# Gated delta-rule attention and mixture of experts: two chains in flight over 16 states, newly ordered engine programs, projection weights split earlier with three buffers

## What is computed

```python
q = short_conv(x @ Wq, conv_q)      # 4 taps, then silu; likewise k and v, three of each per token and head
beta = 2.0 * sigmoid(x @ Wb); g = -exp(A_log) * softplus(x @ Wa + dt_bias)
q = l2norm(q) * d ** (-0.5); k = l2norm(k)
def step(S, (qt, kt, vt, bt, gt)):  # one token; S is 128 x 128 for each sequence and head
    S = S * exp(gt)
    for i in range(3):
        kS = kt[i] @ S
        S = S + bt[i] * outer(kt[i], vt[i] - kS)
    return S, qt @ S
o = o * rsqrt(mean(o * o) + 1e-05) * rms_weight * silu(x @ Wg)
x = layernorm(x + o @ Wo);  x = layernorm(x + experts(x))
```

## Time and profile before

| | us |
|---|---|
| median of 3 runs (lowest, highest) | 5084.51 (5080.6, 5097.39) |
| the profiled execution, its own time | 5080.19 |
| its span | 5078.4 |
| of it setup, up to the barrier | 132.1 |
| of it middle loop, up to the experts' first transfer | 3959.6 |
| experts | 986.7 |
| busy: PE, PEld, DVE, ACT, POOL | 4474.4, 3959.6, 3659.4, 3570.6, 1354.3 |

### The profile page before, as it was taken

One profiled execution on the slowest core, in us unless ns is written; L12 is line 12 of the kernel. 1 busy time (PEld: TensorE's weight loads), 2 busy tenths in 40 slices (PEclk: granted clock), 3 DMA queues, 4 the chain that ended last, 5 costly groups with the idle time before them and its releaser, 6 DMA issues. The chain is left out here.

```text
span 5078.4 us, 150544 instructions
## 1 busy us (share of the span) xinstructions
PE 4474.4 (88%) x50436; PEld 3959.6 (78%) x50436; DVE 3659.4 (72%) x9814; ACT 3570.6 (70%) x8898; POOL 1354.3 (27%) x1231
## 2 busy tenths in 40 slices
PE   1799999999999999999999999999999966599991
PEld 0688888888888888888888888888888845488881
DVE  3788888878888878888888888788888722344445
ACT  2688888878888878888878888778888711255551
POOL 2223333333333333333333333322222202200004
PEclk6999999999999999999999999999999988699996
DMA  4322222222222322222222222222222123366663
GB/s 196 85 59 71 71 74 80 78 70 74 72 72 72 81 69 82 72 72 72 80 70 82 72 72 71 74 63 65 57 57 57 35 84 106 120 234 234 234 232 114
DMA packets 322317, 474.05 MB, mean 93 GB/s; under 512 B 85888, under 2 KB 267136, under 8 KB 302720
## 3 DMA queue, kind: packets, MB, share of 16 engines
q1 hardware_dynamic: 304784, 437.06, 29.4%
q0 software_dynamic: 6144, 16.79, 1.0%
q10 hardware_dynamic: 10608, 10.23, 0.6%
HBM read 352.02 MB, written 107.75 MB: 91 GB/s over the span
## 5 line engine op out<-in xcount | busy, mean ns | idle before, releaser
L1087 DVE SCALAR_TENSOR_TENSOR conv_acc<-bank,c_cur,conv_acc 128x256 f32<-128x256 f32 x2688 | 1283.0, 477 | 23.4 <-ACT conv_acc L899 4.2
L611 PE MATMUL bank<-x_cur,w_cur 128*128 128x259 f16 (+1 forms) x6144 | 855.4, 275 | 69.5 <-DMA g_cur<-g_parts 66.0
L957 ACT ACTIVATE inv<-bank 128x256 f16<-128x256 f32 x1536 | 606.8, 395 | 262.2 <-PE bank L704 241.0
L1258 POOL TENSOR_TENSOR squares<-kq_t 128x1024 f32<-128x1024 f32 x128 | 242.3, 1893 | 1704.6 <-ACT kq_t L911 1704.6
L1144 DVE CAST_PREDICATED xs_lev<-mask,bank 128x256 f16<-128x256 uint16 x1536 | 657.9, 428 | 53.4 <-PE bank L693 5.7
L611 PEld LDWEIGHTS bank<-x_cur,w_cur 128*128 128x128 f16 (+1 forms) x6144 | 588.4, 102 | 137.3 <-DMA g_cur<-g_parts 66.9
L755 PE MATMUL bank<-state,kq_t 128*128 128x128 f32 x2048 | 472.7, 313 | 136.2 <-DVE state L1157 107.6
L1251 POOL TENSOR_TENSOR decay<-decay_tok,cst 128x512 f32<-128x512 f32 x256 | 319.3, 1268 | 948.3 <-ACT decay_tok L923 948.3
L965 ACT ACTIVATE invt<-bank 128x256 f16<-128x256 f32 x1280 | 509.0, 398 | 24.2 <-PE bank L719 0.8
L899 ACT ACTIVATE conv_acc<-bank,c_cur 128x256 f32<-128x256 f32 x896 | 420.7, 469 | 143.2 <-PE bank L611 143.2
L1157 DVE SCALAR_TENSOR_TENSOR state<-state,t_cur,bank 128x128 f32<-128x128 f32 x1024 | 351.3, 343 | 217.5 <-PE bank L777 213.5
(11 more groups left out here) (249 smaller groups left out, 11045.7 us busy)
## 6 DMA issues: line engine op xcount, KB each, us to landing
w_cur<-w_parts_scratch SPq DMA_DIRECT2D x128, 1024.0 KB, 6.8
ew<-e_parts_scratch SPq DMA_DIRECT2D x117, 896.0 KB, 6.2
x_cur<-x_parts_scratch SPq DMA_DIRECT2D x128, 259.0 KB, 7.0
x_slots<-no_rows SPq DMA_DIRECT2D x128, 256.0 KB, 6.3
e_parts_scratch<-e_pair SPq DMA_DIRECT2D x96, 224.0 KB, 3.9
y_scratch<-y_buf SPq DMA_DIRECT2D x128, 128.0 KB, 3.3
y_in<-y_scratch SPq DMA_DIRECT2D x32, 512.0 KB
rows<-x_slots SPq DMA_DIRECT2D x39, 256.0 KB, 5.4
```

Source lines behind the costliest of these rows:

```text
L611: last = mm(bank[c % 2][:, 0:PW], w_cur[res][:, wp, k, c * P:(c + 1) * P].bitcast(BF16 if wp else F16), x_cur[res][:, xp, k, 0:PW].bitcast ...
L957: a(half(inv[g][:], l, 0), packed(halves(bank[4 + g]), l), ACT.Copy).then_inc(t_kept, 1)
L1087: v.scalar_tensor_tensor(acc, bank[c % 2][:, i:i + TB], c_cur[res][:, c, i:i + 1], acc, ALU.mult, ALU.add).then_inc(tap_step if i < TAPS - ...
```

## The change

- The blocks come in another order: all 16 heads of both sequences for a stretch of 256 tokens, then the next stretch. `state` becomes 16 states, so two blocks behind one another belong to different states. A block's chain now spans three bodies: chunks 0 to 2 in the body of stage b, chunks 3 to 7 in the next, and the last update in the one after. In each body two chains are in flight, in two banks of PSUM.
- The bodies of all engines are laid out anew. Group 0 of the inverse begins in the body of stage a, group 1 lies half a body behind. The semaphores now count by lists that follow these orders (`Count`).
- The load of the joint logarithm and exponential table at the body's head is gone; the four users of it (`key_ln`, `key_root`, `var_ln`, `var_root`) and `exp_decay` lie at four places of the body.
- The inverse is kept with a minus sign on the identity (POOL's `minus_one`, new), which makes the identity matmuls of `residual` and `fix` unneeded; `keep_fix` moves from ACT to DVE and adds twice `invt`. Level 0 is a product with a mask in place of a predicated copy.
- The output is copied out (`keep_out`, ACT), squared and summed with the queries' squares by POOL (`out_square`, `out_sum`, new), so `variance` is one matmul in place of two.
- Setup: three buffers for the weights, and ACT's casts of heads 0 to 5 stand between the steps of the gate tables' chain; 6 and 7 stay behind it.
- The experts are the same but for the order in which they read the blocks.

```diff
-RING = 3
-UNROLL = 24
+CHANNELS = (1, 2, 3, 0, 4, 5, 6, 7)
+UNROLL = 32
+WR = 3
...
+                    for h in range(4):
+                        weight_high(h)
                     act.wait_ge(dv, 2)
                     nc.scalar.activation(beta[0:96], work_a[0:96], ACT.Exp).then_inc(ac, 1)
+                    weight_high(4)
...
-            state = sb("state", [P, P], F32)
+            state = sb("state", [P, B * H, P], F32)
...
-                            mm(flat, ident16[:], rep16[:].rearrange("p a b -> p (a b)"), start=True, stop=False)
-                            mm(flat, negid16[:], inv[g][:].rearrange("p a b -> p (a b)"), start=False, stop=False)
...
-                        nc.scalar.preload_act_table_set("natural_log_exp_and_others")
-                        exp_decay()
-                        root_variance()
-                        key_norms()
...
+                        keep_first(1, k1)
+                        var_ln(k3)
+                        silu(5, k1)
+                        keep_t(3, 0, k1)
...
+                        silu(0, k0)
+                        var_root(k3)
+                        exp_decay(k0)
+                        keep_w(5, k2)
+                        silu(4, k0)
+                        keep_w(0, k1)
+                        keep_tt(4, 1, k1)
+                        key_ln(k0)
...
+                    def keep_fix(g, k):
+                        done(dve, x_made, ("fix", g), k.n)
+                        v.scalar_tensor_tensor(inv_t[k.i % R_INV][:, 4 * g:4 * g + 4].rearrange("p a b -> p (a b)"),
+                                               invt[k.i % R_LEV][g][:].rearrange("p a b -> p (a b)"), 2.0, LEVX[:],
+                                               ALU.mult, ALU.add).then_inc(x_kept.sem, 1)
...
-                            v.copy_predicated(half(first[g][:], 0, 1),
-                                              half(mask_sb[:, 0, None, :].broadcast_to([P, 4, P]), 0, 1).bitcast(U16),
-                                              half(n_high[g][:], 0, 1)).then_inc(l0_made, 1)
+                        v.tensor_tensor(half(first[g][:], 0, 1), half(n_high[k.i % 2][g][:], 0, 1),
+                                        half(mask4[:, 0], 0, 1), ALU.mult).then_inc(first_made.sem, 1)
```

More of the change, by code:

```diff
@@ L16 @@
+import math
 from contextlib import ExitStack
@@ new lines, in blocks, with at_stage, g, run_bodies @@
+            def blocks(i, m, size):
+                return [Block(i, m, s, size) for s in range(STAGES)]
+            def at_stage(f):
+                def g(*args):
+                    if args[-1].runs:
+                        f(*args)
+                return g
+            def run_bodies(eng, body):
+                assert NIT % UNROLL == 0 and UNROLL >= STAGES
+                for i in range(UNROLL):
+                    body(*blocks(i, None, UNROLL))
+                with eng.Fori(1, NIT // UNROLL) as m:
+                    for i in range(UNROLL):
+                        body(*blocks(i, m, UNROLL))
+                for i in range(NIT, NIT + STAGES - 1):
+                    body(*blocks(i, None, UNROLL))
@@ new lines, in _ @@
+                    load(0, 0, 0)
+                    for head in range(B * H):
+                        body(0, head)
+                        pieces(0, head)
+                        load_next(0, head)
+                    with sp.Fori(1, NTB - 1) as tb:
+                        for head in range(B * H):
+                            body(tb, head)
+                            pieces(tb, head)
+                            load_next(tb, head)
+                    for head in range(B * H):
+                        body(NTB - 1, head)
+                        pieces(NTB - 1, head)
+                        if head + 1 < B * H:
+                            load_next(NTB - 1, head)
@@ new lines, in level_t @@
+                    @at_stage
+                    def level_t(l, g, k):
+                        done(pe, x_kept, (l, g), k.n)
+                        if l > 1:
+                            done(pe, tt_kept, (l - 1, g), k.n)
+                        free(pe, t_made, t_kept, (l, g), k.n)
+                        by = first[g] if l == 1 else invt[k.i % R_LEV][g]
+                        for u in range(4):
+                            last = mm(packed(LEVT[:, u * HP:(u + 1) * HP], l), by[:, u], half(xs_lev[g][l - 1][:, u], l, 0),
+                                      start=True, stop=True)
+                        last.then_inc(t_made.sem, 1)
@@ new lines, in fix, with from_state @@
+                    @at_stage
+                    def fix(g, k):
+                        done(pe, tt_kept, ("residual", g), k.n, (LEVELS - 1, g))
+                        free(pe, x_made, x_kept, ("fix", g), k.n)
+                        for u in range(4):
+                            last = mm(LEVX[:, u * P:(u + 1) * P], xs[g][:, u], invt[k.i % R_LEV][g][:, u], start=True, stop=True)
+                        last.then_inc(x_made.sem, 1)
+                    @at_stage
+                    def from_state(c, k):
+                        if c % 4 == 0:
+                            done(pe, x_kept, ("fix", c // 4), k.n)
+                            done(pe, rows_kept, ("keys", c // 4), k.n, ("values", c // 4))
+                        if c == 0:
+                            pe.wait_ge(zeroed, 1)
+                            done(pe, stated, 7, k.n - 2)
+                        else:
+                            done(pe, stated, c - 1, k.n)
+                        mm(chain(k), kq_t[k.i % R_KQ][:, c].rearrange("p a b -> p (a b)"), state[:, k.i % (B * H)],
+                           start=True, stop=True).then_inc(ks_made.sem, 1)
@@ new lines, in keep_res, with keep_w, keep_out @@
+                    @at_stage
+                    def keep_res(g, k):
+                        done(act, tt_made, ("residual", g), k.n)
+                        a(xs[g][:].rearrange("p a b -> p (a b)"), LEVTT[:], ACT.Copy).then_inc(tt_kept.sem, 1)
+                    @at_stage
+                    def keep_w(c, k):
+                        done(act, sol_made, c, k.n)
+                        a(w_sol[k.i % 2][:], chain(k), ACT.Copy).then_inc(sol_kept.sem, 1)
+                    @at_stage
+                    def keep_out(k):
+                        done(act, sol_made, 7, k.n)
+                        at_least(act, normed, k.n - 1)
+                        at_least(act, osq_made, k.n - 1)
+                        a(o_raw[k.i % 2][:], outputs(k), ACT.Copy, scale=1.0 / OUT_SCALE).then_inc(out_kept, 1)
```

1499 lines of the change are left out of this document (752 added, 747 removed).

## The result

The changed kernel takes 5157.97 us (median of 4 runs, 5121.88 to 5161.06), the kernel before 5082.56 beside it: ratio 1.0127, interval 1.0078 to 1.0177. It is slower by some 75 us, outside the predicted range, on the side that had 24 in 100. The profiled execution took 5161.06 us, 168 more than the 4992.7 that the prediction's sum gave for one.

A forecast was written before the change was run, and what follows sets the result against it. The prediction took PE to bound the kernel before and ACT, with six table loads, after. From 5080.2 us, setup -41.5, loop end -8 and loop -38 gave 4992.7, so 4997 us as median; range 4820 to 5150.

The forecast's parts named there:

- 1161.7 + 127 P: Whole kernel: fixed parts 1161.7 us plus 127 bodies of P us each, with P taken as 30.2.
- What bounds the kernel: Loop: PE sets the body before; afterwards ACT is fullest, busy 28.5 us a body against PE's 27.1.
- two stalls: Loop body: PE waits behind table loads, update(1) for keep_w(1) 1.4 us, level_x(4,0) for keep_t(3,0) 1.8 us.
- the walk: One body followed through the new orders: ACT leg 21.6 us and PE leg 8.6, together 30.2.
- The price of the loads: ACT in the loop: each table load costs 1.39 us with lost overlap; four more make +5.6 us a body.
- The typical body: Loop: a body takes 30.2 us instead of 30.50, 0.3 less, -38 us over 127 bodies.
- Setup: Before the loop: casts of heads 0 to 5 between the chain's steps save 41.5 us, ends -31 and -41.5.
- the late load: Setup: a load coming late lets ACT's cast hold up the chain, losing up to 10 us.
- End of the loop: After the last exp_decay: 54 us against 62.0, -8, including five links of the chain alone at 2.7 each.
- Contention: Loop: POOL and DVE hold each other up, ACT leg gains about 1.4 us, body 31.6, 5175 us; 24 in 100.
- Hidden loads: Loop: table loads are hidden, ACT runs without pause, body 28.7 us, 4807 us; 13 in 100.
- The chain still sets the body: Loop: bodies stay at 30.5 us, only setup and end are won, 5035 us; 8 in 100.

The follow-up runs named there:

- no_w: The changed kernel with 64 KB of weights loaded per block instead of 1 MB from the second stretch of tokens on: 5052.77 us, ratio 1.0001 to the kernel before.
- load_later: The changed kernel with SP issuing the next block's loads only after PE's Gram matrices of group 0: 5064.74 us, ratio 1.0016 to the kernel before.
- unroll128: The changed kernel with all 128 bodies written out on PE, ACT and DVE, no loop turns: 5094.33 us, ratio 1.007 to the kernel before.
- four_loads: The changed kernel with the joint table loaded ahead of key_ln and var_root, four table loads per body instead of six: 4788.26 us, ratio 0.9474.
- before_six: The kernel before without its joint table load at the body's head, six table loads per body instead of two: 5728.27 us, ratio 1.1316.
- two_b: The changed kernel with silu(4) moved into the next body, four convolution buffers and one joint load, two table loads per body: 4853.01 us, ratio 0.958.
- setup_only: The kernel before with only the changed setup (three weight buffers, casts between the gate tables' steps): 5032.85 us, ratio 0.9935.
- norm_later: The changed kernel with four table loads per body and DVE's normalize moved behind right_side(0): 4776.65 us, ratio 0.9437 to the kernel before.
- unroll16: The changed kernel with 16 bodies per loop turn instead of 32, 7 turns instead of 3: 5299.33 us, ratio 1.0479 to the kernel before.

## Why the prediction was wrong

The forecast was faster with 4997 us; the kernel is slower. Of the 168 us between the sum and the profiled execution:

| term | forecast | measured | us |
|---|---|---|---|
| loop's first load | 90.6 | 101.04 | +10.4 |
| to the first `exp_decay` | 24.3 | 19.7 | -4.6 |
| typical body, times 127 | 30.2 | 30.6 | +51 |
| mean body over the typical one | not in the sum | 0.68 | +86 |
| end of the loop | 54 | 68.9 | +15 |
| experts and what lies around the span | 988.5 | 999.2 | +11 |

- **The step that failed** is the formula "1161.7 + 127 P", into which P went as walked through one undisturbed body. It has no term for PE's instructions coming late, nor for the clock that falls behind such a wait. The mean of the kernel before, 30.50, hid little of that (the median distance there is 30.33, with the excess at the loop's turns), and I took it as none. SP's move of the 1 MB load was never priced, though the prediction should have: it says what each moved step costs, and names no DMA of the loop. no_w and load_later take 72 and 67 of the 86 us away; most of the rest is the turns. Without the 86 the median would have been 5158 - 86 = 5072 us, inside the range and no change. That wasn't the forecast either: the other terms have 82 us.
- **The Trainium skill** ("Runtime: NRT & Kernel Launch", Instruction fetch mechanics) says that the sequencer fetches the next block of instructions by itself and that crossing a block's end is mostly hidden, while a taken branch breaks the prefetch. The runs agree with the second (a body in which a turn falls is 8 to 14 us longer) and not with the first: instructions come up to 5 us late in the straight list of unroll128 too, if a large transfer runs beside many short matmuls. That it is the fetch is shown by the packets of the instruction queue.
- **What bounds the kernel**: right. ACT became the fullest engine with six loads per body, 90% busy; PE fell to 88%, and its two stalls lie where the walk put them, 1.37 and 0.87 us for 1.8 and 1.4.
- **The price of the loads**: right in kind, perhaps a little high (at least 1.25 each in four_loads for 1.39). The 2.66 us a switch of the Trainium skill ("ScalarE: Activation LUTs", What ACT_TABLE_LOAD costs), which the prediction set aside for its row, does not show after either: `ln_v` ends at 3464.73, a load runs from 3464.75, and the silu behind it starts at 3466.04, 1.31 us in all. The 5.2 us a body of before_six can't decide it, with 5.9 us to spare on ACT and a lower clock. "Without the four added loads PE's list would close the cycle at about 27.1" was too good: with two added loads 28.1, with none (two_b) 28.5; another cycle lies just below.
- **The typical body**, 0.4 us long, is within what a walk gives. It turned 0.3 us of gain into 0.1 of loss: the forecast of a gain in the loop stood on a difference smaller than the walk's error.
- **Setup**: -31.1 us for -41.5, at the low end that the text gave, but for another reason than the late load that it named. The exponentials start at 83.78 us, 10.4 later than the 73.36 of the earlier trace rows: the transposition in front of them is 6.4 us later (45.44 for 39.02) by the three casts beside POOL, and the operations at 71.91 add 3.9. The prediction took the chain's end as unchanged; it looked for the contention with POOL in the loop only.
- **End of the loop**: the five links of the chain alone were put at 2.7 us. The first three `from_state` of it, and two windows (the clock is the third number from the end):

```profile
4135.07 0.49 PE L816 MATMUL bank<-state,kq_t 128*128 128x128 f32 x2 [0.54 <-DVE state L1212]
4138.10 0.77 PE L816 MATMUL bank<-state,kq_t 128*128 128x128 f32 x2 [0.53 <-DVE state L1212]
4142.13 0.80 PE L816 MATMUL bank<-state,kq_t 128*128 128x128 f32 x2 [0.44 <-DVE state L1212]
```

```profile
4120.00:4137.00 17.00, 12.97 (x118) 10.63 (x118) 8.51 (x22) 9.25 (x22) 2.59 (x4) 1.00 0.02 8
4138.00:4160.00 22.00, 12.08 (x34) 8.40 (x34) 3.67 (x10) 6.54 (x11) 2.74 (x4) 0.50 0.02 7
```

  The first link, for the most part at the level of 2.4 GHz, is 3.0 us, the others at 1.2 GHz are 4.03 to 4.07; the sum had no fall of the clock. With it the chain and what follows take 26.8 us for 21.5. The other 10 of the 15 us lie before: the chain stands alone from 4135.07 us, 10 later than the forecast's 12 + 20 us behind the last `exp_decay`, so they lie in the rest of that body and the inverse levels of the last block.
- **Experts**: not a change. That stretch differs from run to run: from the experts' first transfer to the end of the span 964.8 us in setup_only, 951.8 in four_loads, 995.8 in the changed kernel's profile.
- **The rivals.** *Contention*, the only slow one, foresaw 5175 us and the time came near, but by luck and not by its mechanism. `normalize` is indeed held up:

```profile
L1219 DVE SCALAR_TENSOR_TENSOR o_norm<-o_raw,neg_rms,rstd x128: 471/1424/1583, 207.3 to 4158.2; 128x256 f32<-128x256 f32 x128
L1165 DVE TENSOR_TENSOR first<-n_high,mask x256: 278/476/1165, 127.6 to 4105.6; 128x256 f16<-128x256 f16 x128
```

  In the median it takes 0.95 us more than its quickest, `first_level` only 0.2. Of that the typical body feels 0.35 us by norm_later, measured with four loads; it may be part of the 0.4 above, which with six loads wasn't tried. *Hidden loads* is refuted by four_loads. *The chain still sets the body* is refuted by the same run: the body falls to 28.1 with the chain unchanged.

## What to carry to other kernels

Walk a body for its typical length, but ask besides where each large transfer is issued, and beside what: if it moves next to TensorE's shortest matmuls, add a term for late instructions, here 0.55 us a body, and look whether the packets of the instruction queue come through beside it. Count ACT's table loads in the new order before anything else; each is about 1.3 us on the fullest engine, and a joint table set takes some away without moving a thing, whereas moving an in-order item to save one can cost as much as it saves. A gain that is smaller than the error of the walk is no forecast: its chance is that of a coin.

## What the runs showed of the hardware

- While the 1 MB of the next block's weights are transferred, TensorE's instruction packets hardly start (5 in 123 blocks from 1 to 5 us after the issue, 51 in 125 if it is 64 KB). If PE starts some 113 matmuls in the 8 us from the issue, it then stands up to 5 us in some of the bodies, from 6 to 11 us after the issue; with the same transfer half a body later and some 75 matmuls it hardly does (issue waits 60 against 10 us).
- Behind such a wait the granted clock falls: a body without a wait of its own read 0.89 and took 34.3 us for 30.6.
- A turn of the loop makes the body in which it falls 8 to 14 us longer (unroll16, load_later). Seven turns of 16 bodies instead of three of 32 also came with more late bodies, 62 for 25, and cost 175 us together.
- DVE's cast of 128 x 128 from SBUF to SBUF, 0.22 us alone, took 4.08 us beside POOL's subtraction of 128 x 2048 (about 4.05 us). The Trainium skill ("SBUF — State Buffer", Practical consequences) says that a cast can take the port shared with GpSimd and that the other blocks fully; here the cast is the one that is blocked, for a whole operation of POOL's, three times in a row. For `normalize` in the loop the mean excess was 0.8 us, less than a whole operation of 1.27.
